# A two-layer adaLN transformer with mixtures of experts: one more pair of sequences is routed, and the order of work is planned with other numbers

## The chip, the cores and the metric

The kernel is one program on one core of a Trainium2 chip. The metric is device time in microseconds (us); a run's time includes some work of the launch around the profiled span. Every engine (PE for matrix products, DVE, ACT, POOL, and SP, which only starts transfers) has its own instruction stream and runs it strictly in the order written; the streams meet through semaphores.

## The reference

Eight sequences of 512 tokens by 128 values go through two layers. Each layer is attention and then a mixture of experts, each behind a layer norm with its own shift, scale and gate per sequence:

```
h = layernorm(x) * (1 + ca) + sa ;  x = x + ga * attention(h)
h = layernorm(x) * (1 + cb) + sb ;  x = x + gb * experts(h)

layer 0 attention: qkv = h @ w_qkv.T, 16 heads of 8, softmax over all 512 keys, output projection + b_out
layer 0 experts:   top 2 of 8, each (silu(t@w1) * (t@w3)) @ w2, hidden 352; plus one shared expert for all tokens
layer 1 attention: q, k, v through a latent of 32, 16 heads of 8, causal mask, projection + b_proj
layer 1 experts:   probs = softmax(h @ Wr); w, idx = top_k(probs, 2)
                   y_e = square(max(h @ W1[e], 0)) @ W2[e] ;  out = sum over e of comb[:, e] * y_e
```

`comb` holds the two chosen weights of a token and zero for the other six experts, so an expert's product may be computed for all tokens and multiplied by `comb`, or for the chosen tokens alone. The two give the same sum. That choice is what the change is about.

## The kernel before

The program counts 16 passes of a sequence through a layer as "sequences": 0 to 7 are layer 0, 8 to 15 are layer 1 of the same eight. Each goes through the same chain: layer norm and projections (steps `p_...`), the row maxima of the scores (`score` on PE, `rowmax` on DVE, for a stabilised softmax), the scores again the other way round (`bscore` on PE L880 and L885, `expo` on ACT), the product with V (`pv`, L897), the output projection (`t_mm`), the second norm (`f_rstd` on POOL, L1596 to L1601, and others), the gate product (`f_gate`, L929), the choice of two experts on DVE (`f_top`, `f_idx`), and the experts. A step `score` or `bscore` is a product of two heads' strips and a small one that adds a code for the head.

**Experts, dense.** The last sequences of layer 1 pass all 8 experts. For each of the 8, PE makes `d_up` (h by W1) and `d_dn` (by W2), ACT the relu and the square (L1532, L1541), DVE multiplies by `comb` (`d_y`, L1343), and POOL adds (`d_add`, L1702). `FD` is the first such sequence, the end of `GROUPS`.

**Experts, routed.** Two sequences (1,024 tokens, 2,048 choices) form a pair, a row of `GROUPS`. Once both have chosen, PE counts the choices by one product (`rr_mm`, L958), DVE works out for each choice a place in a buffer in HBM, sorted by expert and padded to whole tiles of 128 (`rr_a`, `rr_pos`, `rr_tex`), and POOL scatters the rows there with 16 indirect DMAs (`r_sc`, L1655): 8 groups of 128 tokens, 2 choices each. The 16 form two chains; each scatter first waits until the one issued two before it has landed. A pair has 23 tiles. SP loads them four at a time (`x_ld`, six loads); the first lines of that step are

```
for m in range(4):
    q.wait_ge(s["r_sc", m], sent(p))
```

so the first load waits until all 16 scatters have landed. PE transposes the four tiles of a load (`x_turn`, L966), and in layer 1 runs on them `x_up` and `x_dn` with weights that were fetched for each tile's expert; ACT copies and squares between (`x_hst`, `x_th`, `x_sq`, `x_y`); SP stores the result. Then POOL gathers the rows of each sequence back with 16 indirect DMAs (`g_ga`, L1679), ACT weighs them (`g_w`), and POOL sums them and adds the residual (`g_x`, L1686 to L1695).

**What sets the order.** `plan()` lists every step with its engine, a duration (`weight`), a due time (`urgency`), what it comes after, and a `lag`, the time from its end until a successor may start. `Plan.settle()` then plays the program once on paper: at every moment an engine takes, of the steps that could start, the one due first; for PE a change between the ways in which its array is split costs a few hundredths (`SWITCHES`). The orders that come out are written into the streams. The due times are a formula of the sequence number plus four tables of numbers (`SHIFT` for all of a family of steps, `LATE` for layer 1, `LAST` for the last three sequences, `NUDGE` per sequence). Two of the lines that give a routed pair its prices:

```
add("POOL", ("r_sc", q, t, c), 1.35, u, [sent[-2], ("rr_pos", q), ...], lag=1.35)
add("SP", ("x_ld", q, L), 0.45, u - 0.2, sent[-4:] + [("x_turn",) + l2], lag=2.5)
```

In the profile, products through the helper `product` have line L771 or L773 whatever step they belong to. In the changed file all lines behind the tables stand 21 lower: x_turn is L987, the scatter L1676, the gather L1700, d_add L1723, f_rstd L1617 to L1622.

Of the kernel before, what the change touches and what calls it, by code (L numbers as in the profile page):

```python
# [1957 lines left out]
```

How the kernel before makes its waits and increments, by code:

```python
    def wait_ge(self, sem, value):  # L66
        if self.seen.get(sem.name, 0) < value:
            self.eng.wait_ge(sem, value)
            self.seen[sem.name] = value
# [694 lines left out]
        @block.tensor  # L764
# [16 lines left out]
            def open_banks(u):
                q.wait_ge(*on("c_ps"))
                for k in emptied[u]:
                    q.wait_ge(*on(*k))
            for u in todo["PE"]:
                k = u[0]
                if k == "c_warm":
                    q.wait_ge(s["c_pool"], 3)
                    warm(WARM[u[1]]).then_inc(s[k], 1)
                elif k in ("p_turn", "f_turn"):
                    w, i = (0, u[1]) if k == "p_turn" else (1, u[1])
                    q.wait_ge(s["c_pool"], 3)
                    q.wait_ge(*on(("p_norm", "f_norm")[w], i))
                    open_banks(u)
                    for t in range(NT):
                        mm = eng.transpose(ps(*u)[:, 128 * t:128 * t + 128], xn[w][:, t, :], ident[:, :])
                    mm.then_inc(s[k], 1)
                elif k == "m_mm":
                    l = u[1]
                    q.wait_ge(*on("m_s2", l))
                    q.wait_ge(*on("m_ld", l))
                    open_banks(u)
                    for c in range(6):
# [4 lines left out]
                elif k == "m_gm":  # L811
                    l = u[1]
                    q.wait_ge(*on("m_s2", l))
                    q.wait_ge(*on("m_ld", l))
# [5 lines left out]
                elif k == "w_mm":  # L820
                    q.wait_ge(*on("ld", "w1"))
                    open_banks(u)
```

## Time and profile before

| what | value |
|---|---|
| time, median of three runs | 1074.13 us (1073.61 to 1080.87) |
| span of the profiled execution | 1051.9 us |
| the median less that span | 22.2 us |
| PE busy | 979.1 us (93%) |
| DVE busy | 821.8 us (78%) |
| ACT busy | 746.4 us (71%) |
| POOL busy | 456.9 us (43%) |
| share of the chain of waits on PE, DVE, DMA, ACT | 55%, 20%, 9%, 6% |

The profile is of one execution. It has no time of its own for the whole run, only its span, so a forecast here is made against the 1051.9 us of the span, and the 22.2 us between it and the median of the runs are put on top as they are. The chain of waits is followed back from the last instruction, at each step to what released it. A row of the timeline has the start, the duration, the engine, the line, the output and the input, and, where the engine had been idle, for how long and what ended that.

### The profile page before, as it was taken

What the parts mean: (1) busy time and instruction counts of PE and PEld (TensorE: products, weight loads), DVE (VectorE), ACT (ScalarE), POOL (GpSimd) and SP (SyncE); (2) the same over time, 40 slices, a digit from 0 to 9 for tenths busy, and PEclk for the clock granted to TensorE, in tenths of its full rate; (3) what the DMA queues carried; (4) which work ended last, traced back from release to release, by engine and by line L of the source; (5) the groups of instructions that cost most, each with busy time, mean ns of one, the idle gap of its engine ahead of it and who ended that gap; (6) DMA issues with size and microseconds to landing.
All of it is one profiled execution on the core that took longest, in us unless ns stands there. A gap on an engine that the chain in (4) does not pass through costs nothing.

```text
span 1051.9 us, 28537 instructions
## 1 busy us (share of the span) xinstructions
PE 979.1 (93%) x11295; PEld 521.8 (50%) x11295; DVE 821.8 (78%) x1657; ACT 746.4 (71%) x1241; POOL 456.9 (43%) x546
## 2 busy tenths in 40 slices
PE   7688887889999999999999999999999989999998
PEld 6211222222655555445656666667665544455566
DVE  6978999976999788678977689777877667577556
ACT  4458775779664777886676775677757897776865
POOL 5220131243215415642443654455544665855564
PEclk9879999999999999999999999999999999999999
DMA  6932444254754685694666787878787767411100
GB/s 178 248 90 67 126 111 119 68 171 138 227 182 122 201 245 162 180 272 140 197 198 199 217 244 243 249 211 260 213 269 223 212 183 190 101 62 65 36 11 21
DMA packets 120500, 174.79 MB, mean 166 GB/s; under 512 B 19912, under 2 KB 84296, under 8 KB 120368
## 3 DMA queue, kind: packets, MB, share of 16 engines
q1 hardware_dynamic: 114112, 159.87, 51.4%
q0 software_dynamic: 5680, 12.33, 4.0%
q8 instruction: 89, 1.46, 0.6%
q10 hardware_dynamic: 576, 0.79, 0.3%
q14 instruction: 43, 0.35, 0.1%
HBM read 114.21 MB, written 58.59 MB: 164 GB/s over the span
## 4 chain that ended last, share of the span: by engine, by line
PE 55%; DVE 20%; DMA 9%; ACT 6%; issue 5%; POOL 3%; SPq 0%; POOLq 0%; DVEq 0%; ACTq 0%
PE ps L771 17%; PE ps L897 12%; DVE nm L1110 10%; PE ps L773 9%; PE ps L880 6%; PE ps L857 6%; DMA gr<-d_y,pos 5%; ACT ES L1445 4%; DMA d_h<-hx,pos 2%; DMA d_h<-r,pos 1%; POOL gr L1679 1%; PE ps L799 1%; ACT xn L1370 1%; PE ps L885 1%; PE ps L862 1%
## 5 line engine op out<-in xcount | busy, mean ns | idle before, releaser
L1110 DVE TENSOR_REDUCE nm<-ps 128x2 f32<-128x1024 f32 (+3 forms) x512 | 503.8, 1017 | 97.5 <-PE ps L862 52.5
L1445 ACT ACTIVATE ES<-ps 128x1024 f32<-128x1024 f32 (+1 forms) x448 | 416.8, 963 | 85.5 <-PE ps L880 52.9
L897 PE MATMUL ps<-ES,VS 128*9 128x512 f32 (+3 forms) x2048 | 221.8, 518 | 2.1 <-DVE hdx L1294 0.9
L857 PE MATMUL ps<-KS,QS 48*128 48x512 bf16 (+3 forms) x1110 | 180.6, 357 | 23.3 <-DVE nm L1110 16.1
L880 PE MATMUL ps<-QS,KS 51*128 51x512 bf16 (+3 forms) x1072 | 172.4, 348 | 17.2 <-DVE nm L1110 8.1
L880 PEld LDWEIGHTS ps<-QS,KS 51*128 51x128 bf16 x1072 | 50.6, 94 | 147.3 <-ACT ES L1445 56.1
L857 PEld LDWEIGHTS ps<-KS,QS 48*128 48x128 bf16 x1110 | 51.4, 95 | 139.1 <-DVE nm L1110 60.6
L1679 POOL DMA_INDIRECT gr<-d_y,pos x80 | 83.5, 1043 | 79.9 <-DMA gr<-d_y,pos 52.8
L771 PE MATMUL ps<-hsT,wst 128*128 128x128 f32 x676 | 95.4, 284 | 1.1 <-DVE rj L1235 0.5
L771 PEld LDWEIGHTS ps<-hsT,wst 128*128 128x128 f32 x676 | 82.2, 191 | 19.9 <-issue 17.0
L1605 POOL TENSOR_TENSOR sp<-sr,sp 128x512 bf16<-128x512 f32 x32 | 37.2, 1175 | 89.7 <-ACT sp L1406 89.6
L897 PEld LDWEIGHTS ps<-ES,VS 128*9 128x9 f32 x2048 | 37.9, 89 | 66.9 <-issue 52.4
L1490 ACT ACTIVATE tx<-ps 128x384 f32<-128x384 f32 x92 | 44.6, 488 | 36.4 <-PE ps L773 23.6
L1655 POOL DMA_INDIRECT d_h<-hx,pos x40 | 40.1, 1003 | 66.0 <-DMA d_h<-hx,pos 32.1
L773 PE MATMUL ps<-hsT,wst 128*32 128x128 f32 x1896 | 63.7, 274 | 2.3 <-DVE rj L1235 1.7
L1655 POOL DMA_INDIRECT d_h<-r,pos x40 | 39.5, 987 | 57.5 <-DMA d_h<-r,pos 43.3
L1702 POOL TENSOR_TENSOR ya<-ya,yS 128x512 f32<-128x512 f32 x35 | 45.1, 1290 | 43.8 <-DVE yS L1343 43.7
L773 PEld LDWEIGHTS ps<-hsT,wst 128*32 128x32 f32 x1896 | 51.5, 110 | 24.4 <-issue 21.4
L1370 ACT ACTIVATE xn<-X,rs 128x128 f32<-128x128 f32 x128 | 52.5, 483 | 14.9 <-POOL rs L1601 11.9
L1609 POOL TENSOR_TENSOR nmp<-nmr,nmp 32x128 bf16<-32x128 f32 x32 | 13.7, 429 | 97.2 <-ACT nmp L1424 96.9
L1454 ACT ACTIVATE US<-ps 128x512 f32<-128x512 f32 x64 | 38.2, 596 | 19.4 <-PE ps L897 18.7
L862 PE MATMUL ps<-codek,codeq 64*128 64x128 bf16 x512 | 51.7, 217 | 0.0
(233 smaller groups left out, 1539.9 us busy)
## 6 DMA issues: line engine op xcount, KB each, us to landing
wst<-we SPq DMA_DIRECT2D x92, 576.0 KB
d_u<-US SPq DMA_DIRECT2D x60, 256.0 KB
KS<-d_k SPq DMA_DIRECT2D x62, 192.0 KB, 4.2
QS<-d_q SPq DMA_DIRECT2D x62, 192.0 KB, 4.9
hs<-d_h SPq DMA_DIRECT2D x25, 256.0 KB, 3.4
d_y<-ys SPq DMA_DIRECT2D x25, 256.0 KB
d_q<-sp SPq DMA_DIRECT2D x16, 384.0 KB
d_k<-sp SPq DMA_DIRECT2D x16, 384.0 KB
```

Of the source, the lines that this page charges most:

```text
L771: return eng.matmul(to, lhsT, rhs, start=start, stop=stop)
L773: mm = eng.matmul(to[r:r + 32, :], lhsT[:, r:r + 32], rhs, start=start, stop=stop, skip_group_check=True)
L857: mm = eng.matmul(psum[:, bank[u][a], c:c + n], QS[m][r:r + KA, pr, 128 * t1:128 * t1 + 128], KS[m][r:r + KA, pr, 0:n], start=True, stop=i ...
L862: mm = eng.matmul(psum[:, bank[u][a], c + n - 128:c + n], codeq[r:r + 64, :], codek[r:r + 64, :], start=False, stop=True)
L880: mm = eng.matmul(psum[:, bank[u][a], c:c + S - q0], KS[m][r:r + KB, pr, 128 * j1:128 * j1 + 128], QS[m][r:r + KB, pr, q0:S], start=True, ...
L897: mm = eng.matmul(psum[32 * a:32 * a + 9, b, q0:S], VS[i % 3][:, j1, 4 * g + a, :], ES[(2 * EXP[i, g, j] + a // 2) % NES][:, a % 2, c:c + ...
L1110: ins = eng.tensor_reduce(nm[f][:, :].rearrange("p (a c) -> p a c", a=2)[:, :, 4 * pr + t1], ps2("score", i, f, pr, t)[:, :, c:c + n], AX. ...
L1370: ins = eng.activation(xn[w][:, t, :], X[:, NT * b + t, :], ACT.Identity, bias=rs[:, m, 2, t:t + 1], scale=rs[:, m, 1, t:t + 1])
L1445: eng.activation(ES[(2 * n + pp) % NES][:, :, 0:w], ps2("bscore", i, f, g, j, pp)[:, :, 0:w], ACT.Exp, scale=SC1 if i >= NB else SC0).then ...
L1655: eng.indirect_dma_start(out=d_h[:, :], out_offset=bass.IndirectOffsetOnAxis(ap=pos[p % 2][:, c, t8:t8 + 1], axis=0), in_=hx[t8 // NT][:, ...
L1679: eng.indirect_dma_start(out=gr[m][:, :], out_offset=None, in_=d_y[p][:, :], in_offset=bass.IndirectOffsetOnAxis(ap=pos[p % 2][:, c, t8:t8 ...
L1702: eng.tensor_tensor(ya[:, :, :], ya[:, :, :], yS[:, :, :], ALU.add).then_inc(s[k], 1)
```

## The change

`GROUPS` gets a sixth row, (10, 2): sequences 10 and 11 become a routed pair, and only 12 to 15 pass all experts (`FD` goes from 10 to 12). All tables of due times have new numbers. The planner's prices change: 21 kinds of steps have durations of their own (`SERVICE`), the time from one engine to the next is a constant by engine (`HANDOFF`, PE 0.32 us instead of 0.43, the others 0.15 instead of 0.2 to 0.28, SP 0.3 instead of 1.8), and a step that ends in a transfer keeps its own lag with 0.3 us on top (`LANDING`) instead of 0.6. The computation of a step is not changed. The number tables are cut here to a line each.

```diff
-GROUPS = ((0, 2), (2, 2), (4, 2), (6, 2), (8, 2))
+GROUPS = ((0, 2), (2, 2), (4, 2), (6, 2), (8, 2), (10, 2))
...
-SHIFT = {"bscore": -0.04, "c": -16.7, "d": 26.54, "early": -28.49, "expo": -16.03, ...
+SHIFT = {
+    "bscore": -0.04, "c": 6.75, "d": -68.49, "early": 3.31, "expo": -5.918, "f": -23.67, "g": -47.781, ...
...
+    "x": [-0.02, 0.009, -0.106, 0.148, 25.654, -118.27],
 }
-TIED = {"early": "p", "v": "t", "stack": "p", "rowmax": "score", "bscore": "expo", "rr": "r"}
+WHOLE = "m", "c", "x", "rr", "r"
+
+
+SERVICE = {"g_w": 0.58, "rr_pos": 2.3, ... "p_lo": 1.12, "g_x": 4.1, "d_add": 1.28, "d_x": 2.92, "r_sc": 1.1, "g_ga": 1.1, "d_rg": 2.4}
...
-    LAG = {"PE": 0.43, "DVE": 0.26, "ACT": 0.28, "POOL": 0.2, "SP": 1.8}
+    HANDOFF = {"PE": 0.32, "DVE": 0.15, "ACT": 0.15, "POOL": 0.15, "SP": 0.3}
...
-    def add(self, engine, key, weight, urgency, after=(), lag=None, mode="full", opens=0, closes=()):
-        lag = self.LAG[engine] if lag is None else lag
-        if lag >= 1.0 or key[0] in self.MOVES:
-            lag += LATER
-        elif engine in ("PE", "DVE", "ACT"):
-            lag += SPARE
...
+    def add(self, engine, key, weight, urgency, after=(), lag=0.0, mode="full", opens=0, closes=()):
+        moves = engine == "SP" or key[0] in ("r_sc", "g_ga", "d_out", "m_ld")
+        lag = (lag if moves else 0.0) + (LANDING if moves else self.HANDOFF[engine])
...
+        self.work[key] = (engine, SERVICE.get(key[0], weight), urgency, after, lag, mode, opens, closes)
...
-LATER, SPARE = 0.6, 0.05
+LANDING = 0.3
```

The orders of the first four pairs hardly move. Three places do. The first is PE around the first transposition of the last routed pair (the product from `ident` and `hs`); the products from `KS,QS` and `QS,KS` are scores, those from `ES,VS` are `pv`. Before (pair of sequences 8 and 9):

```order
L897 MATMUL ps<-ES,VS 9x384 x4
L880 MATMUL ps<-QS,KS 128x512 x2
L885 MATMUL ps<-codeq,codek 128x128 x2
L966 MATMUL ps<-ident,hs 128x128 x4
L880 MATMUL ps<-QS,KS 128x384 x2
```

And in the changed kernel (pair of 10 and 11):

```order
L918 MATMUL ps<-ES,VS 9x128 x4
L878 MATMUL ps<-KS,QS 128x128 x2
L883 MATMUL ps<-codek,codeq 128x128 x2
L878 MATMUL ps<-KS,QS 128x256 x2
L883 MATMUL ps<-codek,codeq 128x128 x2
L987 MATMUL ps<-ident,hs 128x128 x4
L878 MATMUL ps<-KS,QS 128x384 x2
L883 MATMUL ps<-codek,codeq 128x128 x2
L987 MATMUL ps<-ident,hs 128x128 x4
L792 MATMUL ps<-hsT,wst 128x128 x4
```

Between the counting product of the pair and its first transposition PE had 114 steps for pair 8, 9, and has 75 for pair 10, 11: 32 `score`, 20 `bscore`, 12 `pv`, 1 `x_up`, 1 `x_dn`, 2 output projections, 1 projection of V, 1 `t_mm`, 4 small transpositions and the counting product itself.

The second place is POOL's last scatters (into `d_h`). Before (pair 8, 9), with gathers (into `gr`) only behind them:

```order
L1655 DMA d_h<-hx,pos 2944x128 x4
L1655 DMA d_h<-r,pos 2944x128 x3
L1609 TENSOR_TENSOR nmp<-nmr,nmp 32x128
L1655 DMA d_h<-r,pos 2944x128 x4
L1596 TENSOR_SCALAR rs<-mv 128x4
L1597 TENSOR_SCALAR rs<-mv 128x4
L1599 TENSOR_TENSOR rs<-rs,half 128x4
L1601 TENSOR_TENSOR rs<-rs 128x4
L1655 DMA d_h<-r,pos 2944x128
L1679 DMA gr<-d_y,pos 128x128 x4
```

Now (pair 10, 11), with gathers for sequence 8 between them:

```order
L1676 DMA d_h<-hx,pos 2944x128 x4
L1630 TENSOR_TENSOR nmp<-nmr,nmp 32x128
L1676 DMA d_h<-r,pos 2944x128 x4
L1700 DMA gr<-d_y,pos 128x128
L1676 DMA d_h<-r,pos 2944x128
L1700 DMA gr<-d_y,pos 128x128
L1676 DMA d_h<-r,pos 2944x128
L1630 TENSOR_TENSOR nmp<-nmr,nmp 32x128
L1700 DMA gr<-d_y,pos 128x128
L1676 DMA d_h<-r,pos 2944x128 x2
L1700 DMA gr<-d_y,pos 128x128 x2
```

The gathers of two pairs now follow the last scatters, where those of one did. The third place is POOL before the second norm of sequence 14 (`f_rstd`, four instructions on `rs`). Before:

```order
L1702 TENSOR_TENSOR ya<-ya,yS 128x512
L1620 TENSOR_TENSOR wo<-w1s,GT 128x128
L1621 TENSOR_TENSOR gbo<-bos,GT 128x128
L1625 TENSOR_TENSOR X<-X,gbo 128x512
L1702 TENSOR_TENSOR ya<-ya,yS 128x512
L1596 TENSOR_SCALAR rs<-mv 128x4
```

Now:

```order
L1700 DMA gr<-d_y,pos 128x128 x2
L1723 TENSOR_TENSOR ya<-ya,yS 128x512 x2
L1707 TENSOR_TENSOR cv<-cv,cw 128x512
L1710 TENSOR_TENSOR cv<-cv,GC 128x512
L1716 TENSOR_TENSOR X<-X,cv 128x512
L1723 TENSOR_TENSOR ya<-ya,yS 128x512
L1744 DMA y<-X 128x4x128
L1617 TENSOR_SCALAR rs<-mv 128x4
```

The last gathers and the sum of sequence 11 now stand ahead of that norm. From the first scatter of pair 10, 11 up to it POOL has 48 indirect DMAs, 28 elementwise instructions over 128 by 512 values, one over 128 by 1024, 5 stores and 17 small instructions.

## Rows read from the trace of the kernel before

**Rows 1.** The page: span, and busy time of each engine.

```profile
span 1051.9 us, 28537 instructions
...
PE 979.1 (93%) x11295; PEld 521.8 (50%) x11295; DVE 821.8 (78%) x1657; ACT 746.4 (71%) x1241; POOL 456.9 (43%) x546
```

**Rows 2.** Stretches: bounds, length, busy time of PE, PEld, DVE, ACT, POOL, clock, DMA share, GB/s.

```profile
0.00:260.00 260.00, 219.70 (x1565) 70.64 (x1569) 220.34 (x346) 172.91 (x242) 69.81 (x117) 0.94 0.47 132
866.00:921.00 55.00, 50.91 (x598) 25.87 (x602) 36.59 (x53) 43.51 (x79) 38.69 (x36) 0.97 0.61 149
921.00:1052.00 131.00, 124.43 (x1475) 73.42 (x1467) 85.38 (x240) 94.29 (x164) 69.35 (x74) 1.00 0.12 38
```

**Rows 3.** Timeline of PE, 906 to 914: `pv`, d_dn, scores, d_up (start, duration).

```profile
906.14 1.05 PE L897 MATMUL ps<-ES,VS 128*9 128x512 f32 x8
907.12 0.23 PE L857 MATMUL ps<-KS,QS 48*128 48x128 bf16 x2
...
911.36 1.16 PE L771 MATMUL ps<-r,hd 128*128 128x128 f32 x8
912.45 0.39 PE L857 MATMUL ps<-KS,QS 48*128 48x512 bf16 x2
...
913.12 1.13 PE L771 MATMUL ps<-hF,r 128*128 128x512 f32 x2
914.18 0.34 PE L857 MATMUL ps<-KS,QS 48*128 48x384 bf16 x2
```

**Rows 4.** Timeline of PE, 819 to 823: first transposition of pair 8, 9, and x_up.

```profile
819.78 0.66 PE L966 MATMUL ps<-ident,hs 128*128 128x128 f32 x4 [0.87 <-DMA hs<-d_h]
820.37 0.34 PE L880 MATMUL ps<-QS,KS 51*128 51x384 bf16 x2
...
821.96 1.06 PE L771 MATMUL ps<-hsT,wst 128*128 128x128 f32 x8
822.95 0.34 PE L880 MATMUL ps<-QS,KS 51*128 51x384 bf16 x2
```

**Rows 5.** Timeline of PE: counting product and first transposition of pair 0, 1; gates of 9 and 11, and the counting product of pair 8, 9.

```profile
209.93 0.19 PE L958 MATMUL ps<-ohb,before 128*128 128x64 bf16 x1 [0.24 <-issue]
...
258.50 0.66 PE L966 MATMUL ps<-ident,hs 128*128 128x128 f32 x4
...
746.20 0.40 PE L929 MATMUL ps<-hF,w1s 128*8 128x128 f32 x8
...
757.12 0.20 PE L958 MATMUL ps<-ohb,before 128*128 128x64 bf16 x1 [0.35 <-DVE ohb L1219]
...
852.18 0.41 PE L929 MATMUL ps<-hF,w1s 128*8 128x128 f32 x8
```

**Rows 6.** Timeline of POOL: first and last of the 16 scatters, pair 0, 1 and pair 8, 9.

```profile
216.62 1.27 POOL L1655 DMA_INDIRECT d_h<-hx,pos  x1 [0.19 <-issue]
...
252.73 0.97 POOL L1655 DMA_INDIRECT d_h<-r,pos  x1 [0.30 <-issue]
...
761.59 1.13 POOL L1655 DMA_INDIRECT d_h<-hx,pos  x1 [6.83 <-DVE pos L1274]
...
809.64 1.10 POOL L1655 DMA_INDIRECT d_h<-r,pos  x1 [0.52 <-issue]
```

**Rows 7.** All 80 scatters (line L1655): time from issue to landing.

```profile
DMA to landing us min/median/max: 2.2/5.0/7.3
```

**Rows 8.** The stretch 895 to 900 (columns as in rows 2).

```profile
895.00:900.00 5.00, 3.41 (x60) 2.07 (x64) 1.72 (x3) 4.13 (x7) 3.97 (x4) 0.76 0.07 17
```

**Rows 9.** Timeline of PE in that stretch: a wait, and what ended it.

```profile
896.59 1.08 PE L773 MATMUL ps<-r,hd 128*32 128x128 f32 x32 [2.27 <-ACT tt L1532]
```

**Rows 10.** The page: costliest groups, POOL's (busy, mean ns, idle before and its releaser).

```profile
L1679 POOL DMA_INDIRECT gr<-d_y,pos x80 | 83.5, 1043 | 79.9 <-DMA gr<-d_y,pos 52.8
...
L1702 POOL TENSOR_TENSOR ya<-ya,yS 128x512 f32<-128x512 f32 x35 | 45.1, 1290 | 43.8 <-DVE yS L1343 43.7
```

**Rows 11.** Timeline of POOL: second norm of sequence 14.

```profile
1004.42 0.24 POOL L1596 TENSOR_SCALAR rs<-mv 128x4 f32<-128x4 f32 x1 [0.93 <-DVE mv L1096]
```

More of the change, by code:

```diff
@@ L95 @@
-TIED = {"early": "p", "v": "t", "stack": "p", "rowmax": "score", "bscore": "expo", "rr": "r"}
+SHIFT = {
[3 rows of a table added]
+}
+LATE = {
+    "bscore": 0.008, "d": 20.231, "expo": 26.159, "f": -14.208, "g": -13.92, "max": -5.48, "p": -63.326, "rowmax": -15.758, "score": 0.02,
+    "stack": -1.13, "t": 31.985, "u": -14.639,
+}
+LAST = {
+    "bscore": -70.249, "d": 73.367, "expo": 0.403, "f": -89.449, "max": -0.938, "p": 12.902, "pv": 14.561, "rowmax": -48.942, "score": -12.494,
+    "stack": -18.262, "t": 30.399, "u": 92.948,
+}
@@ L98 @@
+WHOLE = "m", "c", "x", "rr", "r"
+SERVICE = {"g_w": 0.58, "rr_pos": 2.3, "max_sub": 0.19, "max_hi": 0.13, "max_mid": 0.18, "f_lg": 0.33, "f_gt": 0.17, "p_norm": 1.53, "f_norm": 1.53, "rr_oh": 0.35, "m_fin": 1.4, "t_w": 2.24, "p_rstd": 1.88, "f_rstd": 1.88, "p_lo": 1.12, "g_x": 4.1, "d_add": 1.28, "d_x": 2.92, "r_sc": 1.1, "g_ga": 1.1, "d_rg": 2.4}
 class Plan:
@@ L105 @@
              "t_st": 0.15, "g_gc": 0.4, "m_st": 0.1}
-    LAG = {"PE": 0.43, "DVE": 0.26, "ACT": 0.28, "POOL": 0.2, "SP": 1.8}
+    HANDOFF = {"PE": 0.32, "DVE": 0.15, "ACT": 0.15, "POOL": 0.15, "SP": 0.3}
     def __init__(self):
         self.work = {}
-    def add(self, engine, key, weight, urgency, after=(), lag=None, mode="full", opens=0, closes=()):
-        lag = self.LAG[engine] if lag is None else lag
-        if lag >= 1.0 or key[0] in self.MOVES:
-            lag += LATER
-        elif engine in ("PE", "DVE", "ACT"):
-            lag += SPARE
-        family, i = key[0].split("_")[0], key[1] if len(key) > 1 else None
-        urgency += SHIFT.get(family, 0.0)
-        if i in range(NB, N):
-            urgency += LATE.get(family, 0.0)
-        if i in range(N - 3, N):
-            urgency += LAST.get(family, 0.0)
-        table = NUDGE.get(TIED.get(family, family))
-        urgency = round(urgency, 3) + (table[i] if table and isinstance(i, int) else 0.0)
-        self.work[key] = (engine, weight, round(urgency, 3), after, lag, mode, opens, closes)
+    def add(self, engine, key, weight, urgency, after=(), lag=0.0, mode="full", opens=0, closes=()):
+        moves = engine == "SP" or key[0] in ("r_sc", "g_ga", "d_out", "m_ld")
+        lag = (lag if moves else 0.0) + (LANDING if moves else self.HANDOFF[engine])
+        family, i = key[0].split("_")[0], key[1] if len(key) > 1 and isinstance(key[1], int) else None
+        urgency += SHIFT.get(family, 0.0)
+        if i is not None:
+            if family not in WHOLE:
+                if i >= NB:
+                    urgency += LATE.get(family, 0.0)
+                if i >= N - 3:
+                    urgency += LAST.get(family, 0.0)
+            urgency += NUDGE[family][i] if family in NUDGE else 0.0
+        self.work[key] = (engine, SERVICE.get(key[0], weight), urgency, after, lag, mode, opens, closes)
     @staticmethod
@@ L140, in settle @@
         left, ready = {}, {}
-        cands = {e: [] for e in self.LAG}
+        cands = {e: [] for e in self.HANDOFF}
         for k, (e, _, _, after, *_) in self.work.items():
@@ L147, in settle @@
                 cands[e].append(k)
-        free = {e: 0.0 for e in self.LAG}
+        free = {e: 0.0 for e in self.HANDOFF}
         banks = {b: 0.0 for b in range(8)}
@@ L151, in settle @@
         held, mode, moved = {}, None, 0.0
-        todo = {e: [] for e in self.LAG}
+        todo = {e: [] for e in self.HANDOFF}
         bank, emptied = {}, {}
```

37 lines of the change are left out of this document (26 added, 11 removed), and 12 rows, old and new, of tables (NUDGE, SHIFT).

## The prediction

> **What bounds the kernel now.** I read first the page's line of engines [rows 1]: PE is busy 979.1 of 1051.9 us, the next engine 78%. PE is the bound, so what the change takes off PE or makes PE wait for is the first thing to price. A mean hides stages, so I read the stretches next [rows 2]: in the first 260 us PE is idle for 40.3 us (260.0 - 219.7), but in the last 131 us it is busy for 124.4, with ACT at 94.3. All that the change adds lies in those last 200 us, where PE has nothing to spare; a wait of PE there is lost. Third, PE's timeline gives prices from start to start (busy times of neighbours overlap) [rows 3, 4], and the timelines of PE and POOL show how long a routed pair is on its way to PE [rows 5, 6].
>
> **Products taken from PE.** Sequences 10 and 11 no longer make 8 d_up and 8 d_dn each. A d_dn lasts 912.45 - 911.36 = 1.09 us, a d_up 914.18 - 913.12 = 1.06 [rows 3]: 16 x 2.15 = 34.4 us gone. Added are the products on the chosen tokens: 1,024 x 2 choices in 23 tiles are 5.75 loads, each with a transposition of 820.37 - 819.78 = 0.59 us, an x_up of 822.95 - 821.96 = 0.99 [rows 4] and an x_dn of equally many products, taken as equal: 2.57 x 5.75 = 14.8, and a counting product of 0.20 [rows 5]: 15.0. Net **-19.4 us** on PE, all of it on the path, since PE is the bound there. The end of the range for it is small: with a d_up at the price of an x_up, 16 x 2 x 0.99 = 31.7 go, net -16.7.
>
> **A wait put in their place.** The first transposition of the pair needs the first load, which waits for all 16 scatters. From the counting product to the first scatter it took 216.62 - 209.93 = 6.7 us for the first pair and 761.59 - 757.12 = 4.5 for the last; from the first scatter to the last 252.73 - 216.62 = 36.1 and 809.64 - 761.59 = 48.1; from there to the transposition 258.50 - 252.73 = 5.8 and 819.78 - 809.64 = 10.1 [rows 5, 6]. Together 48.6 and 62.7 us. For the last pair the order had 114 PE steps in between, and PE waited only 0.87 us at the transposition [rows 4]. For the new pair 75 steps stand there. Priced by rows: 52 score and bscore steps at 0.33 (two of them lie between 912.45 and 913.12), 12 `pv` at 907.12 - 906.14 = 0.98 [rows 3], six products of about 1.0 and four small transpositions at 0.59 with the counting product: 17.2 + 11.8 + 6 + 2.6 = 37.6 us. Strips beside the causal diagonal are narrower, so I take 35, and 33 as the lower end. The bounds of the stall are 48.6 - 37.6 = 11 and 62.7 - 33 = 30; I take 55 on the way, the middle, as the interleaved POOL work is of the kind that stood between the scatters of both: **+20 us**. SP's queue stands behind this too: the load's wait holds the second half of the stack of sequence 15, which PE needs only later; I price that at nothing, covered by the score work of 13 and 14 that is in order behind the transposition. If that cover is gone it shows as one more wait of a few us, inside the bound of 30.
>
> The reason for the early place is in the prices of the plan: 1.1 us for a scatter and 1.35 + 0.3 for its landing, 2.5 + 0.3 for the load, while the 80 scatters took 5.0 us to land in the median [rows 7]. By the shortest landing, 2.2 us, 8 steps of a chain of two take 8 x (1.0 + 2.2) = 26 us from first to last, and with 5.6 before (the mean of 6.7 and 4.5) and 5.8 behind it is 37 us: then PE would wait 37 - 35 = 2 or 3. The Trainium skill, "DMA: Bandwidth & Descriptors", section "Anatomy of one DMA — SWDGE (gpsimd) path", gives a fixed cost of about 2.0 us and a term in bytes, for 64 KB an estimate of 2.15 us; by that rule the wait would be the small one and the time that of rival A. The median of the rows disagrees with it and only their minimum agrees.
>
> **The clock after a wait.** In 895 to 900 the granted clock is 0.76 [rows 8] where PE had waited 2.27 us for ACT [rows 9], against 1.00 in the stretch behind [rows 2]. A stall of 20 us in the middle of dense work is likely to be followed by the same at a larger size: some us at the lower level of 1.2 GHz, so **+2 us**, between 0 and 6. The Trainium skill, "TensorE: Matmul & The Clock Gate", section "HAM oscillation — how this bites in real kernels", says the same of idle gaps, that the array restarts at half rate; by it the term is surely not 0.
>
> **ACT.** A routed pair puts copies and squares on ACT and takes off relus and squares of the dense form, but later: from the point with the same PE work left (921 us) ACT has 164 instructions with 94.3 us before [rows 2], and 201 in the new order, at 94.3/164 = 0.575 each 115 of about 126 us. That is no bound yet, but small waits of PE grow with it: **+3 us**, between 0 and 8. DVE loses 16 multiplications and gains the few steps of the count; it has 85.4 of 131 there [rows 2] and I price it at nothing.
>
> **The rest of the new numbers.** They reorder the first 850 us by a few steps, counted on PE between each pair's counting product and its transposition: 41, 64, 58, 51 steps before, 39, 72, 55, 53 now. I price that at 0, with a gain as rival B.
>
> Sum against the span: 1051.9 - 19.4 + 20 + 2 + 3 = 1057.5; with the 22.2 us around it 1079.7. **Forecast 1080 us, no change** (+0.5% of the median). Here about 1%, 10.7 us, can be told from no change. Its own range is from the bounds: stall 11 and clock and ACT 0 give 1051.9 - 19.4 + 11 + 22.2 = 1066, the upper end of the stall with the rest as taken gives 1090.
>
> **Rival A, the scatters land fast.** The stall is 3 us instead of 20, the clock and ACT terms 0 and 3: 1051.9 - 19.4 + 3 + 3 + 22.2 = 1061. For it: less DMA runs late in the program (share 0.12 behind 921 us, 0.61 before) [rows 2]. Against it: the first pair, under a share of 0.47, took 36.1 us for its scatters.
>
> **Rival B, the new order fills the early idle time.** If half of PE's 40.3 us [rows 2] go, 20 us come off the forecast: 1060. For it: all tables are new, and hand-overs are priced lower. Against it: the orders of the first four pairs are nearly the old ones, and the start is bounded by DVE (220.3 of 260, as busy as PE) [rows 2].
>
> **Rival C, slower: POOL becomes the bound of the end.** Place: the second norm of sequence 14, which POOL made at 1004.4 us, 47.5 before the end [rows 11]. The first scatter of the new pair comes as long after the last gate product as for the pair before, 761.59 - 746.20 = 15.4, so at 852.18 + 15.4 = 867.6 [rows 5, 6]. From there to that norm POOL has 48 indirect DMAs at 1.04 = 50 us, 28 elementwise instructions at 1.29 = 36 [rows 10], and 23 others, 0.2 to 2.4 us each, some 14: 100 us, so 967.6 without a wait. POOL waited 79.9/80 = 1.0 us before a gather [rows 10]. With 48 of these it is at 1015.6, and with waits of 1.25 before each of ten d_add (43.8/35) [rows 10] at 1028. In the forecast the norm is due at 1057.5 - 47.5 = 1010, so it decides from (1010 - 967.6)/48 = 0.9 us of waiting per indirect DMA. By 1020, between these, the end is 1020 + 47.5 + 22.2 = **1090**, and by 1028 it is 1098. For it: the gathers of two pairs and the dense sums share one in-order stream, and POOL's d_rg waits for the pair's last x_dn. Against it: interleaved, one wait covers another.
>
> **Chances.** Forecast 0.44; A 0.13; B 0.15; C 0.28. Faster by over 1% (below 1063.4) is most of A and B: 0.20. Slower by over 1% (above 1084.9) is C but for its lower part, 0.20, and the upper third of the forecast, 0.14: 0.34. Within 1%: 0.46. The range leaves out at most the lower half of A and B and the top of C: 1058 to 1098; the forecast's own is 1066 to 1090.
>
> **What would show it.** In the changed profile the first transposition of sequences 10 and 11 has a wait for its load (DMA, `hs` from `d_h`) of 11 to 30 us; under 5 us A is right. PE's busy time should be near 960 us (979.1 - 19.4). The clock row of the slice behind the wait should be under 1.00. The second norm of sequence 14 should start 47 or 48 us before the end with a wait for DVE; with POOL busy until then and PE waiting for it, C is right. PE's idle time in the first 260 us should still be near 40 us; near 20, B is right. I am wrong altogether if PE's wait there is small and the span still as long: then something between 870 and 1000 that I priced at nothing, the SP queue first, has taken the gain.

## Result and profile after

The changed kernel takes **1103.63 us** (median of 4 runs, 1099.89 to 1109.54), against 1073.87 for the kernel before in the runs beside it: ratio **1.0273**, 95% interval 1.0227 to 1.032, so 29 us slower. The forecast was 1080, the range 1058 to 1098; "slower by over 1%" had a chance of 0.34. Ratios here leave out three executions that ran over 1.5% longer than the quickest of their kernel (one each of `e7_quarter_dense` and `e8_products_back`, one of the kernel before beside `e4` to `e6`); the medians keep them.

The profiled run took 1099.89 us with a span of 1098.0, so only 1.9 us lie around the span. The execution of the kernel before on which the prediction rests, with its span of 1051.9 [rows 1], was thus an uncommonly quick one: the same kernel profiled again (`e10_before_again` below) ran in 1071.64 us with a span of 1069.7, and in its 73 timed executions beside the other runs the span was 1066.1 us or more and the time 1.9 to 2.1 us longer. Stages are compared with that second profile from here on. First the page of the changed kernel (span, engines, the chain of waits by engine, the groups of [rows 10]), then the same lines of the kernel before, profiled again:

```profile
span 1098.0 us, 26769 instructions
...
PE 992.0 (90%) x10328; PEld 522.8 (48%) x10328; DVE 818.7 (75%) x1659; ACT 745.5 (68%) x1249; POOL 480.1 (44%) x570
...
PE 36%; DVE 16%; DMA 15%; issue 12%; POOL 10%; ACT 10%; another core or an unknown queue 1%; SPq 0%; POOLq 0%; DVEq 0%; ACTq 0%
...
L1700 POOL DMA_INDIRECT gr<-d_y,pos x96 | 100.1, 1042 | 85.1 <-DMA gr<-d_y,pos 52.7
```

```profile
span 1069.7 us, 28537 instructions
...
PE 990.0 (93%) x11295; PEld 524.5 (49%) x11295; DVE 823.6 (77%) x1657; ACT 747.3 (70%) x1241; POOL 457.3 (43%) x546
...
PE 56%; DVE 21%; ACT 8%; DMA 6%; issue 6%; POOL 2%; SPq 0%; another core or an unknown queue 0%; DVEq 0%; POOLq 0%; ACTq 0%
```

PE is not less busy, although by the prediction's prices 19.4 us of products went: 992.0 us against 990.0. Its idle time is 1098.0 - 992.0 = 106.0 us against 79.7. In the chain that ended last PE's share falls from 56% to 36%, and DMA's and POOL's rise to 15% and 10%. The stretches say where (columns as in [rows 2]); changed kernel, then before, profiled again:

```profile
0.00:250.00 250.00, 215.32 (x1418) 68.49 (x1418) 213.58 (x331) 164.56 (x230) 69.59 (x115) 0.90 0.49 132
650.00:850.00 200.00, 182.93 (x2425) 118.22 (x2426) 145.81 (x327) 124.74 (x228) 92.22 (x108) 0.99 0.73 214
850.00:950.00 100.00, 78.94 (x857) 38.09 (x859) 66.96 (x147) 65.50 (x123) 58.96 (x66) 0.89 0.58 160
866.00:921.00 55.00, 45.85 (x482) 22.70 (x480) 43.51 (x106) 34.84 (x68) 32.06 (x37) 0.88 0.64 184
908.00:917.20 9.20, 5.54 (x45) 2.13 (x42) 8.98 (x13) 1.18 (x2) 4.80 (x5) 0.62 0.51 159
```

```profile
0.00:250.00 250.00, 209.73 (x1443) 67.67 (x1445) 209.97 (x329) 159.82 (x225) 66.83 (x113) 0.92 0.46 128
650.00:850.00 200.00, 187.29 (x2924) 121.26 (x2922) 143.94 (x331) 133.22 (x240) 92.86 (x106) 0.99 0.74 221
850.00:950.00 100.00, 94.36 (x1222) 51.29 (x1222) 70.01 (x139) 83.97 (x156) 72.77 (x74) 1.00 0.61 161
```

Up to 850 us the two are nearly level: PE is busy for 781.1 us of them against 782.4, and the first scatter of the fifth pair starts at 774 us in the one and at 780 in the other. Between 850 and 950 PE is busy for 78.9 us against 94.4, at a granted clock of 0.89 against 1.00. In 908 to 917.2 the clock is 0.62, near the lower of its two levels (1.2 of 2.4 GHz), and **DVE is busy for 8.98 of the 9.2 us**. PE there, where [rows 3] had d_dn, scores and d_up in turn:

```profile
909.23 0.23 PE L878 MATMUL ps<-KS,QS 48*128 48x128 bf16 x2 [1.13 <-DVE nm L1131]
909.30 0.22 PE L883 MATMUL ps<-codek,codeq 64*128 64x128 bf16 x2
909.36 0.27 PE L878 MATMUL ps<-KS,QS 48*128 48x256 bf16 x2
909.47 0.22 PE L883 MATMUL ps<-codek,codeq 64*128 64x128 bf16 x2
910.37 0.50 PE L878 MATMUL ps<-KS,QS 48*128 48x384 bf16 x2 [0.67 <-issue]
910.66 0.31 PE L883 MATMUL ps<-codek,codeq 64*128 64x128 bf16 x2
911.29 0.61 PE L878 MATMUL ps<-KS,QS 48*128 48x512 bf16 x2 [0.32 <-DVE nm L1131]
911.69 0.31 PE L883 MATMUL ps<-codek,codeq 64*128 64x128 bf16 x2
912.16 0.29 PE L878 MATMUL ps<-KS,QS 48*128 48x128 bf16 x2 [0.15 <-DVE nm L1131]
...
918.98 1.76 PE L918 MATMUL ps<-ES,VS 128*9 128x512 f32 x8
```

PE waits 0.15 to 1.13 us before most of the score steps, mostly for `nm`, DVE's row maxima, and a score of 0.39 us takes 0.61 at the lower clock, a `pv` 1.76 instead of 1.05. DVE in the same stretch, and in the kernel before (profiled again) in the like place:

```profile
905.47 2.13 DVE L1131 TENSOR_REDUCE nm<-ps 128x2 f32<-128x1024 f32 x3
908.22 8.95 DVE L1131 TENSOR_REDUCE nm<-ps 128x2 f32<-128x768 f32 x12 [0.61 <-PE ps L883]
917.09 0.54 DVE L1145 RECIPROCAL DC<-DC 128x64 f32<-128x64 f32 x1
```

```profile
908.54 0.69 DVE L1343 TENSOR_TENSOR yS<-ps,comb 128x512 f32<-128x512 f32 x1 [1.00 <-POOL ya L1702]
909.15 1.01 DVE L1110 TENSOR_REDUCE nm<-ps 128x2 f32<-128x256 f32 x2
911.03 0.96 DVE L1110 TENSOR_REDUCE nm<-ps 128x2 f32<-128x768 f32 x1 [0.86 <-PE ps L862]
911.90 0.68 DVE L1129 TENSOR_TENSOR OT<-OT,DR 128x512 f32<-128x512 f32 x1
913.26 2.15 DVE L1110 TENSOR_REDUCE nm<-ps 128x2 f32<-128x1024 f32 x3 [0.68 <-PE ps L862]
916.14 0.69 DVE L1343 TENSOR_TENSOR yS<-ps,comb 128x512 f32<-128x512 f32 x1 [0.72 <-PE ps L773]
916.96 0.96 DVE L1110 TENSOR_REDUCE nm<-ps 128x2 f32<-128x768 f32 x1
```

In the changed kernel twelve maxima run without a gap for 8.95 us (a merged row names the shape of its first): here DVE sets the pace. Before, DVE was mostly the one that waited, for PE (`<-PE ps`), since PE had the dense products of 10 and 11 to do between the scores.

These 9.2 us are not all of it. Over the whole 850 to 950 DVE is less busy than before (66.96 us against 70.01), and of PE's 21.1 us of idle time there 6.8 ended with ACT's exponentials and 7.1 with maxima. The longest waits of PE in these bounds (total, times, longest; "issue" means that the profile names no releaser):

```profile
PE ps L901 <- ACT ES L1466: 5.8, 5, 1.6
PE ps L878 <- DVE nm L1131: 5.2, 8, 1.7
PE ps L878 <- issue: 4.2, 4, 2.7
```

The second place is the pair's way to PE and back, with the counting product and the first transposition (as [rows 5]), and POOL's scatters and second norm of sequence 14 (as [rows 6, 11]):

```profile
895.03 0.20 PE L979 MATMUL ps<-ohb,before 128*128 128x64 bf16 x1
...
952.58 0.66 PE L987 MATMUL ps<-ident,hs 128*128 128x128 f32 x4
```

```profile
899.51 1.14 POOL L1676 DMA_INDIRECT d_h<-hx,pos  x1 [4.55 <-DVE pos L1295]
...
938.61 0.42 POOL L1630 TENSOR_TENSOR nmp<-nmr,nmp 32x128 bf16<-32x128 f32 x1 [7.95 <-ACT nmp L1445]
...
942.04 0.98 POOL L1676 DMA_INDIRECT d_h<-r,pos  x1 [0.30 <-issue]
...
1052.60 0.25 POOL L1617 TENSOR_SCALAR rs<-mv 128x4 f32<-128x4 f32 x1
```

From product to transposition it is 57.6 us (the prediction took 55), but no stall stands in front of the transposition; over the whole run PE waits for the pair loads for 0.3 us. From the first scatter to the norm it is 153 us, and the norm starts 45.4 us before the end.

### The profile page after: what moved, and what is told of

It reads as the page before. It is cut to its first block, busy times and chain, and to the rows that moved or that the text cites. A ratio compares the mean times of both kernels' runs of the same rounds, so it can differ in the third digit from the quotient of the medians.

```text
span 1098.0 us, 26769 instructions
## 1 busy us (share of the span) xinstructions
PE 992.0 (90%) x10328; PEld 522.8 (48%) x10328; DVE 818.7 (75%) x1659; ACT 745.5 (68%) x1249; POOL 480.1 (44%) x570
## 4 chain that ended last, share of the span: by engine, by line
PE 36%; DVE 16%; DMA 15%; issue 12%; POOL 10%; ACT 10%; another core or an unknown queue 1%; SPq 0%; POOLq 0%; DVEq 0%; ACTq 0%
PE ps L792 11%; PE ps L918 9%; DVE nm L1131 7%; DMA gr<-d_y,pos 6%; ACT ES L1466 6%; PE ps L901 5%; PE ps L878 5%; DMA d_h<-r,pos 3%; PE ps L794 3%; DMA d_h<-hx,pos 3%; POOL gr L1700 3%; POOL d_h L1676 2%; POOL ya L1723 1%; DVE st L1112 1%; PE ps L820 1%
## 5 line engine op out<-in xcount | busy, mean ns | idle before, releaser
L918 PE MATMUL ps<-ES,VS 128*9 128x512 f32 (+3 forms) x2048 | 229.1, 535 | 4.8 <-DVE hdx L1315 4.2
L878 PE MATMUL ps<-KS,QS 48*128 48x512 bf16 (+3 forms) x1110 | 183.4, 365 | 30.8 <-DVE nm L1131 19.6
L901 PE MATMUL ps<-QS,KS 51*128 51x512 bf16 (+3 forms) x1072 | 176.2, 356 | 31.5 <-ACT ES L1466 20.1
L1700 POOL DMA_INDIRECT gr<-d_y,pos x96 | 100.1, 1042 | 85.1 <-DMA gr<-d_y,pos 52.7
L792 PE MATMUL ps<-hsT,wst 128*128 128x128 f32 x922 | 127.4, 283 | 3.1 <-DVE sr L1124 1.1
L878 PEld LDWEIGHTS ps<-KS,QS 48*128 48x128 bf16 x1110 | 52.8, 96 | 155.1 <-DVE nm L1131 63.8
L792 PEld LDWEIGHTS ps<-hsT,wst 128*128 128x128 f32 x922 | 111.4, 191 | 26.1 <-issue 19.6
L1676 POOL DMA_INDIRECT d_h<-hx,pos x48 | 48.2, 1003 | 61.3 <-DMA d_h<-hx,pos 34.9
L1676 POOL DMA_INDIRECT d_h<-r,pos x48 | 47.6, 991 | 58.6 <-DMA d_h<-r,pos 41.8
L1630 POOL TENSOR_TENSOR nmp<-nmr,nmp 32x128 bf16<-32x128 f32 x32 | 13.5, 423 | 115.2 <-ACT nmp L1445 114.8
L1391 ACT ACTIVATE xn<-X,rs 128x128 f32<-128x128 f32 x128 | 52.6, 486 | 12.3 <-POOL rs L1622 11.6
L906 PE MATMUL ps<-codeq,codek 64*128 64x128 bf16 x512 | 50.5, 220 | 0.3 <-issue 0.2
L1535 ACT ACTIVATE ys<-ps 128x256 f32<-128x256 f32 (+3 forms) x60 | 24.8, 413 | 33.2 <-PE ps L794 15.1
L1617 POOL TENSOR_SCALAR rs<-mv 128x4 f32<-128x4 f32 x32 | 7.8, 244 | 74.2 <-DVE mv L1117 73.2
```

Of the source, the lines that this page charges most:

```text
L792: return eng.matmul(to, lhsT, rhs, start=start, stop=stop)
L878: mm = eng.matmul(psum[:, bank[u][a], c:c + n], QS[m][r:r + KA, pr, 128 * t1:128 * t1 + 128], KS[m][r:r + KA, pr, 0:n], start=True, stop=i ...
L901: mm = eng.matmul(psum[:, bank[u][a], c:c + S - q0], KS[m][r:r + KB, pr, 128 * j1:128 * j1 + 128], QS[m][r:r + KB, pr, q0:S], start=True, ...
L906: mm = eng.matmul(psum[:, bank[u][a], c:c + 128], codek[r:r + 64, :], codeq[r:r + 64, :], start=False, stop=True)
L918: mm = eng.matmul(psum[32 * a:32 * a + 9, b, q0:S], VS[i % 3][:, j1, 4 * g + a, :], ES[(2 * EXP[i, g, j] + a // 2) % NES][:, a % 2, c:c + ...
L1391: ins = eng.activation(xn[w][:, t, :], X[:, NT * b + t, :], ACT.Identity, bias=rs[:, m, 2, t:t + 1], scale=rs[:, m, 1, t:t + 1])
```

## Experiments

Ratios are against the kernel before in the runs beside each, with 95% intervals; 0.01 is 10.7 us.

**The pair alone.** The kernel before with one edit.

```diff
-GROUPS = (..., (8, 2))
+GROUPS = (..., (8, 2), (10, 2))
```

> The kernel before with the sixth pair alone; its tables and prices stay. In the changed kernel the choice of sequence 10 was kept on DVE at 887 us, right behind the last weighing of sequence 7's gathered rows (885.8), although its gate was done at 831: places and weights of a pair lie in two buffers, so a pair's choice waits for the gathers of the pair two before. Theory 1 (that wait makes the pair late, and PE runs out of work that doesn't depend on DVE or ACT): in the order before, the gathers of sequence 7 were weighed by 853 and the gate of 11 was at 852, so the pair is late by little, first scatter near 870; the time stays under 1085. Theory 2 (the low prices of the new plan make its order tight all over; the pair itself is a gain): under 1070. Theory 3 (the pair itself costs, as the dense products of 10 and 11 were the work that filled PE's waits): 1090 or more.

Measured 1128.9 us, ratio 1.0486 (1.0414 to 1.0557), as theory 3 has it. The pair alone does harm, in an order whose due times were made for five pairs; the changed kernel's new numbers leave less of it.

**The plan alone.** The changed kernel without the sixth row.

```diff
-GROUPS = (..., (8, 2), (10, 2))
+GROUPS = (..., (8, 2))
```

> The changed kernel with five pairs; its tables and prices stay, sequences 10 and 11 pass all experts. Theory 1: without a sixth pair nothing waits for the gathers of sequence 7, so the time is near the kernel before, 1074 to 1085. Theory 2: the tight order stays, 1090 to 1105. Theory 3: as theory 1, about 1074. The tables were made for six pairs, so some us above 1074 say nothing.

1095.24 us, ratio 1.0209 (1.0138 to 1.028). Due times made for six pairs cost 2% with five, so this run alone doesn't say what the new prices are worth; the next one but one does.

**A third buffer for weights and places.** In the changed kernel the choice of a pair waited longer than priced. ACT's weighing of sequence 7's gathered rows and DVE's step that keeps the choice of sequence 10 (the gate product was at 830.4):

```profile
885.76 0.42 ACT L1457 ACTIVATE cv<-gr,wts 128x128 f32<-128x128 f32 x1
886.06 0.42 ACT L1457 ACTIVATE cw<-gr,wts 128x128 f32<-128x128 f32 x1
```

```profile
887.47 0.48 DVE L1216 COPY ohs<-lg 128x32 f32<-128x32 f32 x2
887.86 0.16 DVE L1217 TENSOR_SCALAR wts<-m 128x8 f32<-128x8 f32 x1
```

`wts` and `pos` have two buffers, so a pair's choice waits for the gathers of the pair two before. The edit gives both a third, and tells the plan of it.

```diff
-            add("DVE", ("r_keep", i), ... ([("g_w", GROUPS[q - 1][0] - 1, NT - 1)] if q > 1 else []))
+            add("DVE", ("r_keep", i), ... ([("g_w", GROUPS[q - 2][0] - 1, NT - 1)] if q > 2 else []))
...
-        wts = [sb(...) for i in range(2)]
+        wts = [sb(...) for i in range(3)]
...
-                    if p > 1:
-                        q.wait_ge(*on("g_w", GROUPS[p - 1][0] - 1, NT - 1))
+                    if p > 2:
+                        q.wait_ge(*on("g_w", GROUPS[p - 2][0] - 1, NT - 1))
```

> The changed kernel with a third buffer for the places and weights of a pair, so that the choice of a pair waits for the gathers three pairs before. Theory 1: the choice of sequence 10 is made near 840 and that of 11 near 860, the first scatter of the pair at about 868 instead of 899.5, and at least 15 of the 30 us come back: 1075 to 1090. Theory 2: the first scatter moves, the time stays within 6 us of 1104. Theory 3: the same, 1098 to 1110.

1111.74 us, ratio 1.0343 (1.0283 to 1.0402): no gain, and a little above the range of theories 2 and 3. The first and the last of the pair's scatters:

```profile
873.71 1.06 POOL L1676 DMA_INDIRECT d_h<-hx,pos  x1 [1.74 <-DVE pos L1295]
...
929.63 1.12 POOL L1676 DMA_INDIRECT d_h<-r,pos  x1 [0.52 <-issue]
```

They begin 26 us sooner and end only 12 us sooner: the wait was real. But the plan was played again with the third buffer, and the orders of DVE, ACT and POOL are others from about 400 us on, so the run doesn't price the wait alone.

**Prices and due times.** Five pairs with the new prices, six pairs with prices set to the durations of the trace (landing 1.0 instead of 0.3, among others), and six pairs with the prices of before; each with due times searched for that case with the planner.

```diff
-GROUPS = (..., (8, 2), (10, 2))
+GROUPS = (..., (8, 2))
...
-LANDING = 0.3
+LANDING = 1.0
```

(the first part in the first run, the second in the second)

> Five pairs, the changed kernel's prices, and due times searched anew for just this case, so that tables made for six pairs are no excuse. Theory 2 (the new prices are too low, and an order planned with them is tight): still 1080 to 1100, with many waits of PE of 1 to 3 us from 0 to 850 us. If only the mismatch of the tables made the kernel with five pairs slow (1095): 1060 to 1075.

1080.13 us (10 runs), ratio 1.0019 (0.9978 to 1.006). The time is at the lower end of theory 2's range, but the ratio can't be told from 1: with due times searched for them the new prices cost nothing that shows.

> Six pairs, due times searched anew, and the prices that the two traces show from one start to the next: a weighing of gathered rows 0.86 us (the plan has 0.58), the choice of experts 1.6 (1.1), r_keep 0.6 (0.25), rr_a 1.5 (0.96), statistics 1.43 (1.19), changes of PE's array 0.08 to 0.11, and 1.0 instead of 0.3 us on top of a transfer's lag. Theory 2: the sixth pair pays once the order has room, 1035 to 1074. Theory 3 (the dense products of 10 and 11 are missed as filling): 1085 or more, with PE waiting between the counting product of the sixth pair and its first transposition.

1115.02 us, ratio 1.0348 (1.0278 to 1.0417).

> Six pairs, the prices of the kernel before, due times searched anew. Theory 2: with the old, dear hand-overs the order has room, so about the kernel before or better: 1055 to 1078. Theory 3: 1090 or more, as the kernel before with the sixth pair alone (1129) was not slow for want of tables.

1097.51 us, ratio 1.0178 (1.0095 to 1.0261). Five orders with six pairs have now cost 1.8 to 4.9%, and better prices didn't bring the better order.

**Fewer dense columns.** The kernel before, with its order, in which the dense products of 10 and 11 cover 128 of 512 tokens.

```diff
+                    w = 128 if i < 12 else S
-                    product(u, ps(*u), r1[:, e, :], hFs[i])...
+                    product(u, ps(*u)[:, 0:w], r1[:, e, :], hFs[i][:, 0:w])...
-                    for t in range(NT):
+                    for t in range(1 if i < 12 else NT):
```

> The kernel before in its own order, but the 32 dense products of sequences 10 and 11 are made for 128 of the 512 tokens (three quarters of that part of the computation left out; every other instruction is kept). That takes 16 x 2.15 x 3/4 = 26 us off PE and adds nothing. If PE is the bound there, as the prediction took it: 1075 - 26 = 1049. Theory 3 (these products fill time in which PE would wait for DVE and ACT or for free PSUM banks, so that taking them off brings little): 1065 or more, with new waits of PE between 860 and 925 us and a granted clock under 1.00 there.

1074.42 us, ratio 0.9976 (0.994 to 1.0013). Some 26 us of PE's products taken off (by the prices of [rows 3]; the busy time of these groups fell by 18 us) bring 2.6 us, with an interval that has zero in it. Where they stood, PE is idle instead and the clock is lower; this kernel, then the kernel before, profiled again:

```profile
880.00:1000.00 120.00, 103.81 (x1275) 50.64 (x1275) 89.00 (x182) 96.32 (x171) 78.03 (x80) 0.94 0.45 121
```

```profile
880.00:1000.00 120.00, 117.00 (x1538) 59.93 (x1534) 87.54 (x171) 96.66 (x169) 75.18 (x79) 1.00 0.40 106
```

**These products filled PE's waits; they didn't set the end.** The waits that came in their place were mostly for ACT's exponentials (850 to 1000 us, this kernel; DVE's maxima ended 2.4 us in all):

```profile
PE ps L880 <- ACT ES L1446: 5.2, 7, 2.1
PE ps L857 <- ACT ES L1446: 2.7, 6, 0.9
```

**Products put back.** 32 unread products of 0.95 us in the changed kernel, between the counting product and the first transposition, and then, instead, 49 score steps of that stretch made twice.

```diff
+    for n, a in enumerate(EXTRA):
+        add("PE", ("z", n), 0.95, -2000.0, [("ld", "r1"), a], mode="any", ...)
...
 MORE_S = {
+    (13, 1, 3, 3): 1, (14, 0, 0, 1): 1, ...
```

> The changed kernel with 32 products that nobody reads (0.95 us each, 31 us in all) put into PE's order between the counting product and the first transpositions of the sixth pair, where PE idled and its clock was at 0.67 to 0.87. If PE is the bound: 1104 + 31 = 1135. Theory 3: within 12 us of 1104, since the products take the place of waits and keep the clock up (granted clock of that stretch 0.95 or more).

1118.91 us, ratio 1.0402 (1.0325 to 1.0479): 0.0129 x 1074 = 14 us more than the change for some 31 us of products, so neither theory's value came (12 us at most, or 31). The plan was played again with these steps, and from about 894 us on the orders of DVE, ACT and POOL are others too; how much of the products found idle time this run can't say.

> The changed kernel in its own order; each of the 49 score and bscore steps that ran between 896 and 951 us is made twice into the same bank (the kernel has a table for that, used for the first sequences), about 14 us of products. If the lower clock is a cause of its own (PE falls behind because it runs at half rate after its waits): the granted clock of 903 to 955 rises from about 0.8 to over 0.93 and the time falls by 5 to 15 us, to 1089 to 1099. If the waits themselves are what costs and the clock only follows: 1100 to 1115.

1113.92 us, ratio 1.0378 (1.0299 to 1.0457), some 11 us more for 14 us of products, though this interval overlaps that of the change; the time is in the range given for waits that cost by themselves. The stretch 903 to 955 in the changed kernel, then with the 32 products, then with the repeats:

```profile
903.00:955.00 52.00, 38.43 (x392) 16.05 (x392) 36.36 (x58) 24.09 (x41) 27.05 (x31) 0.80 0.56 149
903.00:955.00 52.00, 50.06 (x454) 23.56 (x447) 24.17 (x41) 25.83 (x42) 16.15 (x19) 1.00 0.48 141
903.00:955.00 52.00, 41.74 (x510) 22.25 (x508) 29.43 (x43) 17.80 (x29) 22.66 (x24) 0.79 0.41 114
```

The repeats didn't lift the clock (0.79, from 0.80), so they don't test what it costs; the 32 products did lift it, to 1.00, and the time rose. The low clock goes along with the waits and isn't shown to be a cause of its own.

**The kernel before, profiled again.** No edit.

> The kernel before, unchanged, for a second profile. The prediction put 22.2 us around the span of 1051.9 us; in the profiles of the other kernels the span is 2 to 6 us below the time. If the first profile was of an uncommonly quick execution, the span here is 1066 to 1076 us with the same order of work, and its first scatter of pair 8, 9 is near 780 instead of 761.6; if the launch does take 22 us, the span is again near 1052.

1071.64 us with a span of 1069.7, shown above.

**POOL's indirect DMAs of the new pair left out.** The 16 scatters, the 16 gathers, and both.

```diff
                 elif k == "r_sc":
                     p, t8, c = u[1:]
+                    if p == 5:
+                        continue
...
                     m = 2 * (n % 4) + c
+                    if p == 5:
+                        continue
```

> The changed kernel without the 16 scatters of the sixth pair (that part is left out; its loads read what the pair before left in the buffer, and every other instruction is kept in its order). Theory 4 (rival C of the prediction: from 900 us on the chain that ends last runs through POOL's indirect DMAs and sums, which stand ahead of the second norm of sequence 14): POOL is rid of the 42 us from 900 to 942, that norm comes 20 to 35 us earlier, 1070 to 1085. Theory 3 alone (PE has nothing to do but scores): 1095 or more.

1093.28 us, ratio 1.0193 (1.0118 to 1.0268), between the two theories' ranges.

> The changed kernel without the 16 gathers of sequences 10 and 11 (left out; the sums use old rows, every other instruction is kept in its order). Theory 4: POOL is rid of 16 x (1.04 + about 0.9 of waiting) = 31 us between 999 and 1042, of which sums fill a part: the norm of sequence 14 comes 10 to 25 us earlier, 1080 to 1095. Theory 3 alone: within 8 us of 1104.

1095.32 us, ratio 1.0177 (1.0118 to 1.0235), again between them.

> The changed kernel without the 16 scatters and the 16 gathers of the sixth pair (both left out). Theory 4: 1050 to 1075, about as quick as the kernel before or quicker, with PE the main part of the chain that ends last again. Theory 3 alone: 1090 or more, and the chain still mostly not PE.

1091.11 us, ratio 1.0147 (1.0097 to 1.0197). So (0.0273 - 0.0147) x 1074 = **13.5 us of the 29 hang on POOL's indirect DMAs and what waits for them** (give or take 7, by the two intervals); half of the loss is still there without any of them, where theory 4 had none left. The same two edits in the better order with six pairs, that of `e6_old_prices_six`:

> The order with six pairs that cost least (e6, 1097.5 us, 1.0178 of before) without the 16 scatters and 16 gathers of sequences 10 and 11: their rows of the sorted copy and of the weighted sums are then stale, all else is done. Theory P: POOL's 32 indirect DMAs and what waits for them are the whole loss of a good order with six pairs; the time is 1070 to 1079 us, ratio 0.997 to 1.005. Theory F: the greater part is PE without the independent products of 10 and 11, its waits and its lower clock; the time stays at 1084 to 1097, ratio 1.010 to 1.021, and PE's mean clock stays below 0.97.

1090.65 us, ratio 1.0132 (1.0088 to 1.0176), mean clock 0.963. Theory P falls: a rest is there in this order too.

**Shorter maxima.** What the rows of DVE suggest, tried in three kernels: the changed one, the one before, and the changed one without the indirect DMAs.

```diff
                     for t1, c, n in ...:
+                        n = n if i < 12 else 64
                         ins = eng.tensor_reduce(nm[f]..., ps2("score", i, f, pr, t)[:, :, c:c + n], AX.X, ALU.max, negate=True)
```

> The changed kernel with DVE's row maxima of sequences 12 to 15 taken over the first 64 keys of each strip instead of all of its 128 to 512 (a shift of the softmax's exponent, the same weights in exact arithmetic). In the changed profile twelve such maxima follow one another without a gap from 908.22 for 8.95 us while PE waits after nearly every score; each becomes about 0.5 us instead of 0.6 to 1.2. Theory D: without the dense products between the scores DVE's maxima set PE's pace at 900 to 950; the time is 1083 to 1096 us, ratio 1.009 to 1.021. Rival P: POOL's chain and the landings alone set the end; the time stays at 1098 to 1106, ratio 1.023 to 1.030.

1092.12 us, ratio 1.0152 (1.0107 to 1.0196): (0.0273 - 0.0152) x 1074 = 13 us off (give or take 7). A shortened maximum took 0.29 us, less than the 0.5 expected, and DVE's busy time fell from 818.7 to 755.4 us. PE's waits for `nm` in front of L878 between 850 and 950 fell from 5.2 to 1.1 us. Its stretch 850 to 950, beside 78.94 for PE and 66.96 for DVE above:

```profile
850.00:950.00 100.00, 83.90 (x940) 44.64 (x941) 36.53 (x153) 70.64 (x131) 62.49 (x70) 0.91 0.67 183
```

> The kernel before with the same shorter maxima of sequences 12 to 15. Theory D: there the dense products of 10 and 11 stand between the scores and DVE waits for PE, so less than 4 us comes off: 1070 to 1076 us, ratio 0.996 to 1.002. Rival: the maxima bound the end in any order, as much comes off as in the changed kernel, 8 to 20 us: 1054 to 1066, ratio 0.981 to 0.993.

1073.83 us against 1077.4, ratio 0.9967 (0.9938 to 0.9996): 3.5 us off for 62 us less work of DVE (823.6 to 761.2), where DVE didn't set the pace.

> The changed kernel without the 16 scatters and 16 gathers of sequences 10 and 11 (their routed rows are then stale), and with the same shorter maxima of 12 to 15. Theory D with POOL's share beside it: of the 15 us that remained without the indirect DMAs most go, 1072 to 1082 us, ratio 0.998 to 1.008. Rival: what remained is something else; 1086 to 1095 us, ratio 1.011 to 1.020.

1079.11 us, ratio **1.002** (0.9991 to 1.0048). Both edits together take back 27 of the 29 us, 13.5 and 13.6, nearly the sum of what each took back alone. All three runs are where theory D put them.

## Why the prediction was wrong

**"-19.4 us on PE, all of it on the path, since PE is the bound there": this step failed.** The 124.4 busy of 131 us [rows 2] was read as work that sets the end. Part of it was work that ran where PE would else have waited for DVE or ACT. With three quarters of the products taken off and nothing else changed the time stayed (`e7_quarter_dense`), PE waiting for ACT instead; and when they went altogether, with their places in the order, DVE's chain of maxima came to the surface as well: 13 us by `e15_short_maxima`, of which the kernel before, too, would gain 3.5 (`e16_short_maxima_before`). The prediction priced DVE "at nothing", on its 85.4 busy of 131 us; the step that should have been made is to look at DVE in the stretch from which the fill is taken, where [rows 3] show scores and dense products in turn. In the old order's 866 to 921 us DVE was busy for 36.59 of 55 us [rows 2]; in the same bounds of the changed kernel it is 43.51. A mean over 100 us would not have shown it, as DVE is no busier there than before.

**"Rival C, slower: POOL becomes the bound of the end"** (0.28) had the sign and a good half of the mechanism. Its length held: 153 us from the first scatter to the norm, where 1016 to 1028 less 867.6 makes 148 to 160. Its start failed: 899.5 instead of 867.6, since the interval was taken from the pair before, and the choice of sequence 10, with its gate product at 830.4, was kept only at 887.5, behind the weighing at 885.76 that frees `wts`; the last gate product came at 853.4, nearly where the prediction had it. With the start 32 us later and 2 us around the span in place of 22.2 it gives 1016 + 32 + 47.5 + 2 = 1097 to 1109, and 1103.6 came. The chain that ended last does run through POOL's scatters, gathers and sums from 899.5 to 1056.7, but its sign, PE waiting for that norm, didn't come: PE was busy for 49.1 of the 52.6 us ahead of it. The agreement of the sum is no proof that POOL alone is the bound: leaving its indirect DMAs out gives back only 13.5 us, and `e17_short_maxima_no_indirect` shows about as much beside it that hangs on DVE's maxima.

**"+20 us" of stall.** The way of 55 us was right (57.6), the form wrong: there is no stall in front of the load but small waits all along, because the 75 steps before it couldn't run at the price of [rows 3]. A scatter stood 7.95 us behind a small POOL step that waited for ACT (the row at 938.61), in the same in-order stream. By the named test, a wait of 11 to 30 us, the forecast is refuted; and a wait of 0.3 us, "under 5 us A is right", does not make rival A right either: PE came late to the transposition, not the load early. That is the case in which the prediction called itself wrong altogether. The suspect that it named first, SP's queue, doesn't show: from 850 us on no more than 0.3 us of waiting on PE ends with a load (4.6 us have no named releaser).

**"+3 us" for ACT, DVE "at nothing".** Both terms were too small. From 850 us on PE waited 14.7 us for ACT, against 3.4 in the kernel before, and 12.5 for DVE, against 4.0.

**"+2 us" for the clock.** Far too small in the trace: the mean clock is 0.961 against 0.980. A rough account, as the mean counts idle time too: 1098.0 x 0.039 = 42.8 us lost to the lower level against 1069.7 x 0.020 = 21.4, so 21 us more. With the 10.9 us between the two profiles of the kernel before (990.0 - 979.1) that is why PE was busy for 992 us and not for the 960 named; with 26.3 us more idle time and 19.4 less work it makes 28.3, the difference of the spans, and that it fits so well is luck. Whether the clock costs anything beside the waits is open, as `e9_repeats` didn't raise it. The Trainium skill, "TensorE: Matmul & The Clock Gate", section "HAM oscillation — how this bites in real kernels", says that the array restarts at half rate behind idle gaps; the trace agrees in sign, the clock being 0.62 where PE was busy for 5.54 of 9.2 us. The prediction placed one gap where many small ones came.

**"22.2 us around the span"** was wrong by 20: it is about 2, and the profiled execution was a quick one; why is not known. In the forecast the two mistakes cancel, as its sum was put on top of a median.

**New prices "at 0", rival B.** Right for the prices (`e4_new_prices_five`, 1.0019); B didn't come: of the 20 us that it wanted, 5.6 went from the first 250 us (PE busy for 215.3 us against 209.7), and by 850 us they were lost again.

**What stays open.** In `e17_short_maxima_no_indirect` the time equals that of before, though 19.4 us of PE's products are gone; against `e16_short_maxima_before` it is still 1079.1 - 1073.8 = 5 us more. Which waits hold that was not tried. In the changed kernel PE's waits for ACT grew more than those for DVE, and no run made ACT quicker: what its exponentials are worth, here and in `e7_quarter_dense`, isn't shown. Nor is it known whether an order exists in which six pairs pay: five were run, none searched with DVE's maxima as the scarce thing.

## What to carry to other kernels

Before you count an engine's removed work as a gain, look in the timeline at what stands between its neighbours: work that sits in the gap between a step and its consumer on another engine can be free there, and taking it out, as in `e7_quarter_dense`, can buy idle time and a lower clock of PE. Prove it cheaply: shrink the work in place, in the old order, and see whether the time moves. And when a step comes once more to a pipeline of double buffers, look for the wait that its two predecessors never showed.
